# A transformer megakernel on one core: the experts' results in four places instead of two, and the first attention's VectorE order, v tiles and x turns rearranged

## The reference

```python
x = x + attn_a(layernorm(x))   # 16 heads of 64, ALiBi slopes, causal softmax, out @ w_out + b_out
x = x + ffn(layernorm(x))      # rms norm, gate: top 2 of 8 experts, swiglu, weighted sum
x = x + attn_b(layernorm(x))   # 8 heads of 128, rotary q and k, causal softmax
x = x + ffn(layernorm(x))      # the same experts again
```

## Time and profile before

| what | value |
|---|---|
| median of 3 runs | 2406.43 us (2403.44 to 2410.53) |
| the profiled execution's own time | 2398.29 us |
| its span, first to last instruction | 2396.4 us |
| busy share PE / DVE / ACT / POOL | 90% / 63% / 61% / 54% |
| mean granted TensorE clock | 0.971 |

### The profile page before, as it was taken

One profiled execution on the slowest core, in us unless ns is written; L12 is line 12 of the kernel. 1 busy time (PEld: TensorE's weight loads), 2 busy tenths in 40 slices (PEclk: granted clock), 3 DMA queues, 4 the chain that ended last, 5 costly groups with the idle time before them and its releaser, 6 DMA issues.

```text
span 2396.4 us, 38394 instructions
## 1 busy us (share of the span) xinstructions
PE 2147.5 (90%) x11652; PEld 1722.1 (72%) x11652; DVE 1503.7 (63%) x4317; ACT 1453.4 (61%) x3769; POOL 1287.8 (54%) x1450
## 2 busy tenths in 40 slices
PE   6898989898989999898996899999999999889993
PEld 5576767677767777676885687777877778667782
DVE  5666666665766666556764656566566664746665
ACT  4776767676767676534442667667576665634443
POOL 3564455555545455466652555665656655447661
PEclk7999999999999999999998999999999999999996
DMA  3230000000000000423341001010010000422426
GB/s 122 89 115 27 1 22 6 15 14 10 19 10 19 10 10 12 164 82 84 109 135 58 18 19 45 10 36 27 19 45 10 18 19 1 189 60 82 157 88 236
DMA packets 55140, 132.34 MB, mean 55 GB/s; under 512 B 12256, under 2 KB 30208, under 8 KB 53920
## 3 DMA queue, kind: packets, MB, share of 16 engines
q1 hardware_dynamic: 37216, 92.58, 10.5%
q0 software_dynamic: 17728, 37.32, 5.3%
HBM read 81.51 MB, written 48.35 MB: 54 GB/s over the span
## 4 chain that ended last, share of the span: by engine, by line
PE 59%; ACT 13%; DVE 10%; POOL 8%; issue 6%; DMA 3%; SPq 0%; ACTq 0%; POOLq 0%; DVEq 0%
PE bank L616 5%; PE bank L638 5%; PE bank L2073 4%; PE bank L600 4%; PE bank L1394 3%; ACT P L759 3%; PE bank L1374 3%; PE bank L585 2%; ACT P L1506 2%; PE bank L2047 2%; PE bank L2048 2%; PE bank L2049 2%; PE bank L586 2%; PE bank L1359 2%; ACT q L750 2%
## 5 line engine op out<-in xcount | busy, mean ns | idle before, releaser
L1096 POOL TENSOR_TENSOR P<-P,rc 128x128 f32<-128x128 f32 (+3 forms) x512 | 356.0, 727 | 389.6 <-DVE rc L925 389.1
L917 DVE CUSTOM_DVE_ANT_0 P<-bank,tab 128x512 f32<-128x512 f32 (+3 forms) x512 | 241.4, 485 | 122.3 <-PE bank L586 117.7
L759 ACT ACTIVATE P<-P,mn 128x128 f32<-128x128 f32 (+3 forms) x512 | 281.5, 552 | 43.8 <-DVE mn L917 40.8
L770 ACT COPY PT<-bank 128x512 f32<-128x512 f32 (+1 forms) x384 | 194.2, 516 | 130.5 <-PE bank L600 122.6
L1860 POOL TENSOR_TENSOR q<-rf,q 128x512 fp32r<-128x512 f32 x128 | 162.5, 1293 | 169.1 <-ACT q L1489 166.2
L1853 POOL TENSOR_TENSOR rf<-rp 128x512 f32<-128x512 f32 x128 | 163.6, 1279 | 164.5 <-DVE rp L1684 162.7
L600 PE MATMUL bank<-cst,P 128*128 128x128 f32 x1280 | 210.7, 280 | 36.3 <-ACT PT L770 19.1
L585 PE MATMUL bank<-q 128*128 128x512 f32 (+3 forms) x512 | 187.1, 376 | 49.6 <-DVE mn L917 29.4
L2277 POOL DMA_INDIRECT yD<-Yf,place x142 | 139.1, 979 | 131.1 <-ACT Yf L2137 118.5
L600 PEld LDWEIGHTS bank<-cst,P 128*128 128x128 f32 x1280 | 153.8, 142 | 68.7 <-POOL P L1096 25.4
L2123 ACT ACTIVATE sgf<-glf 128x256 f32<-128x256 f32 x142 | 59.3, 417 | 202.4 <-DVE glf L2194 202.4
(11 more groups left out here) (230 smaller groups left out, 6026.2 us busy)
## 6 DMA issues: line engine op xcount, KB each, us to landing
hD<-hh SPq DMA_DIRECT2D x16, 512.0 KB, 2.6
W1lf<-w1lD SPq DMA_DIRECT2D x2, 4096.0 KB, 13.1
yg<-yD SPq DMA_DIRECT2D x14, 512.0 KB, 4.3
X<-in_x SPq DMA_DIRECT2D x8, 512.0 KB, 4.6
stage<-in_w SPq DMA_DIRECT2D x8, 512.0 KB, 3.6
w1hD<-W1A SPq DMA_DIRECT2D x8, 512.0 KB, 2.6
w1lD<-stage SPq DMA_DIRECT2D x8, 512.0 KB, 3.6
rD<-xn SPq DMA_DIRECT2D x8, 512.0 KB, 2.9
```

The source lines that it names most:

```text
L759: i = e.activation(ps, ps, ACT.Exp, bias=mn[:, pb, t:t + 1], scale=-1.0, accum_out=rs[:, pb, t:t + 1])
L770: e.copy(PT[:, h % 2, PTO[cs[0]]:PTO[cs[0]] + w], bank[4 + n % 2][:, 0:w]).then_inc(q.a_pt, 1)
L917: e.tensor_tensor_reduce(out=P[:, pb, OFF[t]:OFF[t] + w], in0=score(h, t), in1=tab[:, 512 - w:512], scale=-SLOPES[h % 16], scalar=3e38, op ...
L1096: i = e.tensor_tensor(ps, ps, rc[:, h % 3, t:t + 1].broadcast_to([128, w]), ALU.mult)
```

## The change

1. Experts, both phases: `Y` has four places, with a semaphore for each, and `y_copy(a)` waits for the scatter of tile a - 4. The rows in DRAM that padding goes to are four times 128 instead of two. The first four `put_ids` of the last batch but one are issued before the first gather, the others with tiles 0 to 3.
2. First attention, PE: v's tiles go by a table, mostly one in a step (steps 1, 1, 2, 3 and 5, 6, 7, 7), all in bank 7. The next x is turned at the end of the first half of steps 1 and 2, in the heads' bank 6. `attend` of steps 1 and 2 waits until VectorE has read that bank (`x_low`).
3. First attention, DVE: `copy_k` directly behind `low` of the second half, ahead of `v_copy` and `residual`. `x_low` in the second half of steps 1 and 2, ahead of `low`. From the second batch on, the next x is normalised in step 0 (`at` 1 to 4), and its statistics are taken in step 7 of the batch before (`at` 70 to 74); `deviation` goes to step 7 with them. `normal(1)` goes from `at` 22 to 25 to 24 to 27.
4. Some semaphores are merged (`v_set`), and waits on bank 7 are adapted; in the last batch `tally` waits for `v_copy` of the v tile ahead of it.

```diff
 def x_bank(bt, kc):
-    return bank[6] if bt == 0 and kc else bank[7]
+    return bank[6] if bt or kc else bank[7]
 def v_bank(g, t):
-    if g == 0:
-        return t % 2
-    return 1 if g % 2 and t == 3 else 7
+    return 7 if g else t % 2
+V_AT = {(1, 0): (1, 0), (1, 1): (1, 1), (2, 0): (1, 2), (3, 0): (1, 3),
+        (5, 0): (2, 0), (6, 0): (2, 1), (7, 0): (2, 2), (7, 1): (2, 3)}
+def v_tile(bt, p, hl):
+    i, t = V_AT.get((p, hl), (0, 0))
+    return (2 * bt + i, t) if i and 2 * bt + i < 2 * NB else None
...
 # tensor, xpose
-if kc and bt:
-    e.wait_ge(q.v_xT, turned(bt, 0))
-elif bt == 1:
-    e.wait_ge(q.v_xT, turned(0, 1))
-elif bt > 1:
-    e.wait_ge(q.v_x1, 2 * bt - 2)
+if bt:
+    e.wait_ge(q.a_o, 8 * bt - 7 + kc)
...
 # tensor, attend
-if u:
+if u % 8 in (1, 2) and u // 8 + 1 < NB:
+    e.wait_ge(q.v_xT, turned(u // 8 + 1, u % 8 - 1))
+elif u:
     e.wait_ge(q.a_o, u)
...
 # tensor, loop
-if u % 4 > 1 and u // 4 + 1 < 16:
-    proj_v(u // 4 + 1, 2 * (u % 4 - 2) + hl)
-if p == 1 and nx:
-    xpose(bt + 1, hl)
+if v_tile(bt, p, hl):
+    proj_v(*v_tile(bt, p, hl))
+if p in (1, 2) and hl == 0 and nx:
+    xpose(bt + 1, p - 1)
...
 # tensor, last batch
-e.wait_ge(q.v_x1, 2 * bt)
+e.wait_ge(v_v, 8 * bt + 5)
 tally(e, 0, 0)
...
 # vector, between
-elif at in (22, 23, 24, 25):
-    normal(1, bt - 1, at - 22)
+elif at in (24, 25, 26, 27):
+    normal(1, bt - 1, at - 24)
...
+elif bt + 1 < NB and at in (1, 2, 3, 4):
+    normal(0, bt + 1, at - 1)
+if bt + 2 < NB:
+    if at in (70, 71, 72, 73):
+        stats(0, bt + 2, at - 70)
+    elif at == 74:
+        gather_stats(0, bt + 2)
...
 # vector, loop
+if p in (1, 2) and hl and nx:
+    x_low(bt + 1, p - 1)
 if u + 2 < NU:
     low(u + 2, hl)
+    if hl:
+        copy_k(u + 2)
+if v_tile(bt, p, hl):
+    v_copy(*v_tile(bt, p, hl))
-if u % 4 > 1 and u // 4 + 1 < 16:
-    v_copy(u // 4 + 1, 2 * (u % 4 - 2) + hl)
-if p == 1 and nx:
-    x_low(bt + 1, hl)
 if p == 0 and bt:
     residual(bt - 1, hl)
...
-if u + 2 < NU:
-    copy_k(u + 2)
...
 # gpsimd
-if p == 0 and bt + 1 < NB:
-    deviation(0, bt + 1)
+if u == 0:
+    deviation(0, 1)
+if p == 7 and bt + 2 < NB:
+    deviation(0, bt + 2)
...
 # experts, scalar
-if a > 1:
-    e.wait_ge(d_y[a % 2], 16 * (ph * ((NS + 1 - a % 2) // 2) + a // 2))
-e.copy(Y[:, a % 2], bank[4 + a % 2][:, 0:D]).then_inc(a_y, 1)
+if a > 3:
+    e.wait_ge(d_y[a % 4], 16 * (ph * ((NS + 3 - a % 4) // 4) + a // 4))
+e.copy(Y[:, a % 4], bank[4 + a % 2][:, 0:D]).then_inc(a_y, 1)
...
 # experts, gpsimd
 scores_over(e)
+for n in range(4):
+    put_ids(e, ph, BL - 1, n)
 gather(e, ph, q, 4)
...
-if a < 8:
-    put_ids(e, ph, BL - 1, a)
+if a < 4:
+    put_ids(e, ph, BL - 1, a + 4)
```

More of the change, by code:

```diff
@@ L68, in program @@
         rD = [dram(f"rD{i}", [NT * 128, D]) for i in range(2)]
-        yD = [dram(f"yD{i}", [PLACES + 256, D]) for i in range(2)]
+        yD = [dram(f"yD{i}", [PLACES + 512, D]) for i in range(2)]
         bD = dram("bD", [2, E * 768])
@@ L442, in attention_a @@
             q = Phase("", 3)
-            v_q, v_v, v_kd, p_xb, v_kz = (sem(n) for n in ("v_q", "v_v", "v_kd", "p_xb", "v_kz"))
-            v_z, v_gw, v_w1 = sem("v_z"), sem("v_gw"), sem("v_w1")
+            v_q, v_v, v_kd, p_xb = (sem(n) for n in ("v_q", "v_v", "v_kd", "p_xb"))
+            v_gw, v_w1 = sem("v_gw"), sem("v_w1")
             d_tab, p_qs = sem("d_tab"), sem("p_qs")
@@ L545, in proj_v @@
                             e.wait_ge(v_v, t - 1)
-                        elif g and v_bank(g, t) == 1:
-                            e.wait_ge(v_q, halves(4 * g + 1, 1))
+                        elif g > 2 and t == 0:
+                            if g % 2:
+                                e.wait_ge(q.v_x1, 2 * bt)
+                            else:
+                                e.wait_ge(q.v_lg, bt - 1)
+                        elif g > 2 and g % 2 == 0 and t == 1:
+                            e.wait_ge(r_op, 2 * bt - 3)
+                        elif g > 1:
+                            e.wait_ge(v_v, 4 * g + t)
+                            if g == 2 * NB - 1 and t == 1:
+                                e.wait_ge(r_tab, 1)
                         elif g and t:
                             e.wait_ge(v_v, 4 * g + t)
[L550 to L558, removed]
                         o, ts = bank[v_bank(g, t)][:], slice(t * 128, (t + 1) * 128)
@@ L645, in gate_turn @@
                             e.wait_ge(q.v_x1, 2 * bt + 2)
-                            e.wait_ge(q.v_xT, turned(min(bt + 2, NB - 1), 1))
                             if bt < NB - 1:
-                                e.wait_ge(v_v, 8 * bt + 15)
+                                e.wait_ge(v_v, 8 * bt + 16)
                         else:
@@ L711, in tensor @@
                                     e.wait_ge(r_st, 1)
+                                else:
+                                    e.wait_ge(v_v, 8 * bt + 9)
                                 rank(e, 0, bt - 1)
@@ L836, in scalar @@
                                     split(n)
-                            if p == 1 and nx:
-                                x_high(bt + 1, hl)
+                            if p in (1, 2) and hl == 0 and nx:
+                                x_high(bt + 1, p - 1)
                             if p == 3 and bt and hl:
@@ L1119, in gpsimd @@
                     e.wait_ge(d_cst, 32)
-                    e.wait_ge(v_mh, 1)
+                    e.wait_ge(v_set, 1)
                     deviation(0, 0)
@@ L1951, in attention_b @@
             return (tensor, scalar, vector, gpsimd, sync), q
-        d_br, v_bz = sem("d_br"), sem("v_bz")
-        d_y = [sem(f"d_y{i}") for i in range(2)]
+        d_br = sem("d_br")
+        d_y = [sem(f"d_y{i}") for i in range(4)]
         a_fx, v_fx, f_up, v_gl, a_sg, v_ac = (
@@ L2276, in scatter @@
                         e.wait_ge(a_y, T0 + a + 1)
-                        e.indirect_dma_start(yD[ph], bass.IndirectOffsetOnAxis(ap=place[:, a:a + 1], axis=0), Y[:, a % 2],
-                                             None).then_inc(d_y[a % 2], 16)
+                        e.indirect_dma_start(yD[ph], bass.IndirectOffsetOnAxis(ap=place[:, a:a + 1], axis=0), Y[:, a % 4],
+                                             None).then_inc(d_y[a % 4], 16)
                     scores_over(e)
+                    for n in range(4):
+                        put_ids(e, ph, BL - 1, n)
                     gather(e, ph, q, 4)
@@ L2298, in all_chosen @@
                 def all_chosen(e):
-                    for k in range(2):
-                        e.wait_ge(d_y[k], 16 * (ph + 1) * ((NS + 1 - k) // 2))
+                    for k in range(4):
+                        e.wait_ge(d_y[k], 16 * (ph + 1) * ((NS + 3 - k) // 4))
                 def sync(e, store):
@@ L2318, in sync @@
                     scores_over(e)
-                    e.wait_ge(v_bz, ph + 1)
+                    e.wait_ge(v_set, ph + 5)
                     for i in range(2):
@@ L2358, in experts @@
                 finals = [(f_dn, T0 + NS), (a_y, T0 + NS), (v_ac, T0 + NS), (v_wlo, 24), (d_wo, 32)]
-                finals += [(d_y[k], 16 * (ph + 1) * ((NS + 1 - k) // 2)) for k in range(2)]
+                finals += [(d_y[k], 16 * (ph + 1) * ((NS + 3 - k) // 4)) for k in range(4)]
                 finals += [(q.d_r, 16 * NB), (q.v_w, 3 * NB)]
```

35 lines of the change are left out of this document (16 added, 19 removed).

## The result

The changed kernel takes **2347.35 us** (median of 4 executions, 2343.16 to 2350.64); the kernel before took 2408.25 beside it. Its profiled execution has a span of 2348.5 us, where before had 2396.4: 47.9 us less, against 49 forecast on that same scale. That the sum is so near is luck in good part: the first attention gave 47 where I said 34, the experts 1 where I said 15, and the two errors nearly cancel.

A forecast was written before the change was run, and what follows sets the result against it. TensorE, busy 90% of the span, bounds the kernel, so only its idle time can be won. Middle batches 30, first batch 4, last 0, experts 15: 49 us off 2406.4 gives 2357 us, range 2344 to 2386.

The forecast's parts named there:

- A middle batch: First attention, each of six middle batches: PE's idle time falls from 9.4 to 5.25 us; 5.0 saved with the clock.
- step 2's POOL wait: First attention, second half of step 2: PE waits 0.55 us for POOL's scale, behind `deviation` and `mean_square`.
- `attend`: First attention, step 2: PE waits 1.05 us before this product, as all four `normal(1)` lie ahead of `x_low`.
- The clock: First attention, middle batches: fewer half-speed stretches behind the smaller waits, 0.9 us taken of 1.4 for each batch.
- The first batch: First attention: the same three waits go and POOL's weight work gives some back, 4 us saved (2 to 7).
- The experts: Both experts' phases: 4.5 + 1.6 + 4.9 + 4.2 = 15 us saved (8 to 23).
- as four places and half as many tiles with three DMAs leave no wait: Experts, six tiles beside the first `put_ids`: 4.5 us go in `experts(0)`, 4.9 in `experts(1)`.
- the 4.2 us of the second stretch in `experts(1)`: Thirteen tiles, 8.8 us over: 2.7 us saved before POOL's rate stops PE, 1.5 for the place waits after.
- POOL, not the places, sets the experts' pace: Experts: tiles with three DMAs stay at 3.83 us, only 5 of the 15 us come, 2367 us; chance 0.12.
- the "nothing": Second `put_ids` stretch of `experts(0)`, 10.9 us too much: no gain counted, PE comes earlier to the same stop.
- The heads' bank: First attention: `x_low` 2.5 us later in steps 1 and 2, middle batches gain nothing, 2387 us; chance 0.12.
- The port rival: First attention: VectorE and POOL obstruct each other, four norms take 0.92 us each ahead of `x_low`, 2364 us; chance 0.06.

The follow-up runs named there:

- experiment 6: The changed kernel with all four second-norm writes (`normal(1)`) behind `x_low`, at 28 to 31, third chip: 2394.57 us, ratio 0.9745 to the kernel before.
- experiment 7: The changed kernel with `deviation(1)` and `mean_square` moved on POOL from step 1 to between step 2's scales, second chip: 2369.24 us, ratio 0.9698.
- experiment 1: The kernel before with the experts' part of the change alone: 2405.85 us, ratio 0.9983.
- experiment 3: The kernel before with `copy_k` alone moved ahead of `v_copy` and `residual`: 2405.81 us, ratio 0.9972.
- Experiment 4: The changed kernel with v's tiles in pairs in steps 2, 3, 6 and 7, with their old banks: 2359.96 us, ratio 0.9782.
- experiment 2: The changed kernel with the experts' part taken back, so the attention's part alone: 2359.86 us, ratio 0.9787.
- Experiment 9: The changed kernel without the last batch's eight `put_ids` in each experts' phase, second chip: 2341.57 us, ratio 0.9584.
- experiment 10: The changed kernel with the third and fourth weight piece ahead of `fetch_ids`, third chip: 2405.91 us, ratio 0.9795.
- experiment 5: The changed kernel with the four second-norm writes two VectorE places later, at 26 to 29, second chip: 2373.66 us, ratio 0.9716.
- experiment 8: The changed kernel with all eight `put_ids` of the last batch but one ahead of the gathers, both phases, second chip: 2371.28 us, ratio 0.9718.
- experiment 11: The changed kernel with the edits of experiment 6, experiment 7, experiment 8 and experiment 10 together, third chip: 2385.79 us, ratio 0.9713.

## Why the prediction was right, and where its terms were not

**A middle batch: right in its mechanism.** Forecast 116.8 us, measured 692.64 / 6 = 115.4. Term by term, measured after the forecast: step 1 0.2 and none, step 2's POOL wait 0.55 and 0.56, `attend` 1.05 and 1.36, step 3 1.0 and 1.02, step 4 1.1 and 1.08, step 5 0.95 and 0.81, step 7 0.2 and 0.06. The idle time left is 30.1 / 6 = 5.0 against 5.25. Experiments 6 and 7 tie the two new waits to their causes: take the norms or the two POOL pieces from their place and the wait goes. Where `attend` waited 0.31 longer than I said, the trace shows the term: from the first maximum to `x_low` VectorE took 4.56 us (546.21 to 550.77) where I had 4.2, and stood 0.48 of it for scores that were behind PE's wait on POOL, of which I had counted 0.2. Without that wait, in experiment 7, `attend` waited 1.05; its norms were 0.5 us shorter in sum as well, and the two are not parted.

**The clock: under-sized.** I took 0.9 of 1.4 us a batch for the half-speed stretches, 5.4 for six. PE's busy time fell by 11.8. Of the ten profiled executions with the new table of v's tiles, eight had none of the lower clock in these batches and two had one stretch of 3.4 us; before, experiment 1 and experiment 3 had 17, 21 and 31 us. Half of before's 17.1 us is 8.6; the remaining 3.2 of the 11.8 I can't place. Experiment 4 brings the lower clock back in its one profile, with the same sum of gaps. That points to the even spread of PE's work as the source of the rest, where I had credited the smaller waits alone; one execution doesn't prove it.

**The first batch: under-sized.** 4 us forecast (2 to 7), 10.6 measured. PE stood 8.3 us against 15.8, and two half-speed stretches are gone. I had expected POOL's weight work to give more back.

**The experts: over-sized, and the rival was right there.** The step that failed is "as four places and half as many tiles with three DMAs leave no wait", and with it the 4.2 us of the second stretch in `experts(1)`. Experiments 1 and 2 price the part at 4 to 7 us, not 15; that is the 5 of the rival "POOL, not the places, sets the experts' pace", and tiles 19 to 30 of `experts(1)` took 3.79 us each, near that rival's 3.83. The places did what was forecast, 48.2 us of landing waits to none. But PE needs each tile's gather too, and those are issued by the same queue of instructions: of the 12.3 us that PE waited less for turned activations, 7.6 came back as waits for Gf. Experiment 9 shows that the third DMA is behind them. In `experts(0)` the "nothing" was right: ACT's wait for the third piece grew from 3.06 to 5.50, and 38.2 us became 38.9. That the piece, and not POOL's pace, is the stop there is argued from the trace; experiment 10 could not test it. Of the two stages PE stood 4.2 us less, and was busy 3.3 longer, as the clock was at its lower level for 5.7 and 5.3 us more: that leaves the 1 us.

**The rivals.** The heads' bank did not take back what it freed (L619 waited under 1.4 us, none in step 1). The port rival: the four norms took 0.38, 0.80, 0.78 and 0.60 us beside POOL's work, some 1 us more in sum than four like the first. The sum held most of that already, since its 4.0 us for the chain came from norms of 0.38, 0.59, 0.57 and 0.92. My reading of those rows was wrong, though: I had said that only the last one stood behind POOL. The first norm began before POOL's scale and was not lengthened; each of the three after it began inside one of POOL's instructions and ended 0.15 us after that instruction's end, before (at 558.99, 559.82 and 560.87 us) as after (the third at 550.11, the scale at 549.96; the fourth at 550.85, POOL's next instruction at 550.70). The rule of the Trainium skill, "SBUF — State Buffer", section "Who interferes with whom", has the later one stand for the other's whole instruction; the trace agrees, and how long a norm stands is what is left of POOL's instruction when it comes.

## What to carry to other kernels

Before counting a removed wait as won, ask what else the waiting engine needs from the same busy queue: 48 us of ACT's landing waits were worth 4 to 7 us on PE, because most of what PE won came back as waits for gathers, which stand in the same queue of GpSimd as the scatters. In a hand-written order, look at what stands directly ahead of the copy that TensorE waits for: norms behind the copy cost PE nothing in experiment 6, the same norms ahead of it 1.4 us in every batch. Spreading filler matmuls evenly may pay through the clock even where the sum of idle time stays the same; here one profiled execution speaks for it.

## What the runs showed of the hardware that was not expected

VectorE's norm can stand far longer beside GpSimd than the 0.92 us of the earlier trace rows. In step 0 of the changed kernel one of the four norms begins 0.2 us behind POOL's scale, whose four instructions follow one another without a break from 506.48 to 509.22, and ends 0.16 us after the last of them:

```profile
506.67 2.71 DVE L882 TENSOR_SCALAR xn<-X,mv,rstd 128x256 f32<-128x256 f32 x1
```

It is so in four of the batches. Where no instruction of POOL was under way the same norm took 0.38 to 0.42 us. Nor does every instruction of POOL do this: norms that began beside an indirect DMA or `mean_square`'s 128x4 piece of 1.04 us took 0.41 in several cases. PE had no wait in that step, so this cost PE nothing; ahead of a copy that PE waits for, it may not.

The chips differ in where the same program waits. Tiles 16 to 30 of `experts(1)` took 53.6 and 52.9 us on the first chip (experiments 1 and 4), 59.4 to 60.1 on the second (5, 7 and 8) and 60.9 to 61.3 on the third (6, 10, 11 and the change itself). So a price taken in the experts on one chip, as in experiments 8 and 9, need not hold on another.

The 25 plain tiles 31 to 55 of `experts(1)` took 75.53 us in the change's own execution and 82.34 in that on the third chip, with the granted clock at 1.00 in both and PE standing 2.9 us of it. Why PE's recorded busy time is 3.9 us longer there, nothing in these traces tells; it is left open.
